# Attention with a three-slot PSUM ring: another order of units, fp32r projections, the rotation as one operation per unit, normalisation on ScalarE

## What is computed

```python
q = (x @ Wq.T + bq)      # 16 heads, two streams of 8 columns each
k = (x @ Wk.T + bk)
v = x @ Wv.T + bv        # 16 heads of 8 columns
q1, q2, k1, k2 = rope of the streams of q and k
a1 = softmax(causal(q1 k1 / sqrt(8))); a2 = softmax(causal(q2 k2 / sqrt(8)))
out = (a1 - lam * a2) @ v
out = out * rsqrt(mean(out * out) + EPS) * head_norm_w * (1 - LAMBDA_INIT)
return out @ Wo.T + bo
```

## Time and profile before

| | |
|---|---|
| median of 3 runs | 1861.6 us (1861.06 to 1861.72) |
| profiled execution: its own time, its span | 1863.3 us, 1861.6 us |
| PE busy (matmul, ends modelled) | 1608.8 us, 86% |
| DVE busy | 1363.2 us, 73% |
| ACT busy | 1269.4 us, 68% |
| POOL busy | 1046.3 us, 56% |
| mean granted TensorE clock | 0.968 of full speed |

### The profile page before, as it was taken

How to read it: one execution, slowest core, us unless ns; L and a number is a source line. 1 busy time by engine, 2 the same in 40 slices (tenths; PEclk the granted TensorE clock), 3 DMA queues, 4 the chain that set the end, 5 groups by cost and what they waited for, 6 DMA issues and landing times. The chain is left out here.

```text
span 1861.6 us, 43161 instructions
## 1 busy us (share of the span) xinstructions
PE 1608.8 (86%) x16448; PEld 1220.1 (66%) x16448; DVE 1363.2 (73%) x3442; ACT 1269.4 (68%) x1613; POOL 1046.3 (56%) x707
## 2 busy tenths in 40 slices
PE   4999999994588888888888888888873799999998
PEld 3787777883466666666666666666652577778787
DVE  5777777765778778878887788788742677777775
ACT  4777777772167767767677677677664577777776
POOL 4888888875324434334344343343312688888885
PEclk9999999997699999999999999999996799999999
DMA  3333323321323233232232332322302232233331
GB/s 113 103 114 115 102 88 108 109 103 46 87 79 92 58 91 82 66 94 72 76 94 61 86 87 60 95 78 70 89 12 77 97 115 90 93 114 110 108 109 63
DMA packets 142846, 163.14 MB, mean 88 GB/s; under 512 B 13244, under 2 KB 124558, under 8 KB 141454
## 3 DMA queue, kind: packets, MB, share of 16 engines
q1 hardware_dynamic: 142640, 160.38, 28.8%
HBM read 91.20 MB, written 14.70 MB: 57 GB/s over the span
## 5 line engine op out<-in xcount | busy, mean ns | idle before, releaser
L292 POOL TENSOR_TENSOR ffn_h_low<-ffn_h,ffn_h_high 128x1024 fp32r<-128x1024 f32 x192 | 458.4, 2401 | 95.0 <-ACT ffn_h_high L341 94.8
L1019 ACT ACTIVATE att_prob<-att_ring 128x1024 f32<-128x1024 f32 x384 | 388.6, 1022 | 155.9 <-PE att_ring L1240 153.4
L1125 DVE TENSOR_REDUCE att_nmax<-att_ring 128x4 f32<-128x1024 f32 (+1 forms) x384 | 450.8, 1217 | 54.3 <-PE att_ring L1240 54.3
L479 DVE TENSOR_TENSOR ffn_h<-ffn_up,ffn_comb_wide 128x1024 f32<-128x1024 f32 x256 | 311.3, 1216 | 125.1 <-ACT ffn_up L334 122.8
L334 ACT ACTIVATE ffn_up<-ffn_up 128x1024 f32<-128x1024 f32 x256 | 258.1, 1008 | 202.8 <-PE ffn_up L567 201.1
L341 ACT ACTIVATE ffn_h_high<-ffn_h 128x1024 fp32r<-128x1024 f32 x256 | 269.3, 1052 | 0.7 <-DVE ffn_h L479 0.7
L935 POOL TENSOR_TENSOR att_qk<-att_turned 128x512 f32<-128x512 f32 x64 | 81.4, 1273 | 318.0 <-DVE att_turned L1104 318.0
L1240 PE MATMUL att_ring<-att_qs,att_kd 64*128 64x256 bf16 (+1 forms) x2048 | 151.1, 249 | 95.4 <-DVE att_nmax L1125 57.2
L567 PE MATMUL ffn_up<-ffn_xt_high,ffn_w_high 128*128 128x512 f32 x512 | 214.7, 419 | 1.7 <-DVE ffn_h L479 1.6
L580 PE MATMUL ffn_y<-ffn_h_high,ffn_w_high 128*128 128x512 f32 x512 | 205.3, 401 | 7.0 <-POOL ffn_h_low L292 6.0
L284 POOL TENSOR_TENSOR ffn_ez<-ffn_e_const,ffn_nz 128x16 f32<-128x16 f32 x64 | 185.6, 2901 | 38.2 <-DVE ffn_nz L405 38.2
(11 more groups left out here) (146 smaller groups left out, 2840.7 us busy)
## 6 DMA issues: line engine op xcount, KB each, us to landing
ffn_comb_wide<-ffn_comb_d SPq DMA_DIRECT2D x128, 512.0 KB, 5.6
att_qs<-att_parts SPq DMA_DIRECT2D x192, 128.0 KB, 2.5
att_kd<-att_parts SPq DMA_DIRECT2D x192, 128.0 KB, 2.5
ffn_x<-x SPq DMA_DIRECT2D x32, 256.0 KB, 3.1
ffn_w<-w SPq DMA_DIRECT2D x4, 1024.0 KB, 7.2
x<-ffn_out SPq DMA_DIRECT2D x16, 256.0 KB, 2.4
att_x<-x SPq DMA_DIRECT2D x32, 128.0 KB, 2.3
att_xr<-x SPq DMA_DIRECT2D x32, 128.0 KB, 2.3
```

The source lines that it names most:

```text
L292: nc.gpsimd.tensor_tensor(hts[1][:, e % NH], h[:, e % NH], hts[0][:, e % NH], ALU.subtract).then_inc(low_by_pool, 1)
L479: nc.vector.tensor_tensor(h[:, e % NH], up[:, e % NUP], comb_wide[:, b.c % NW, e].unsqueeze(1).to_broadcast([P, HE, FT]), ALU.mult).then_i ...
L1019: nc.scalar.activation(prob[:, u % NP], ring[:, ORDER.index((kind, u)) % 3], ACT.Exp, scale=SCALE).then_inc(prob_ready, 1)
L1125: nc.vector.tensor_reduce(nmax[:, b, :, h0:h0 + cnt], ring[:, pos % 3] .rearrange("p (s h k) -> p s h k", s=2, k=width), AX.X, ALU.max, ne ...
```

## The change

It does six things, all in the attention.

1. `ORDER` and the table `AFTER` are written anew. S0, S1 and S2 now stand among XT, QK0 and QK1, NM comes behind S2, OP is last.
2. The projections of q, k and v are three fp32r products each (high x high, high x low, low x high: `PRODUCTS`) in place of one fp32 product. The weights are split once at the start; xt is split in every turn, its high part by ScalarE's copy, its low part by a new VectorE subtraction behind XT.
3. VectorE's rotation is one operation per unit (no bias).
4. The bias, already rotated, lies in `biased`, made once by VectorE at the start, and GpSimd adds it in a second addition behind rotate.
5. ScalarE normalises x, as Identity with scale and bias; VectorE makes the shift (minus mean times rstd) for it.
6. GpSimd's rstd also waits for the normalisation of the turn before, and waits for the new semaphores are added.

```diff
-ORDER = [("XT", 0), ("T", 6), ("QK", 0), ("NM", 0), ("QK", 1), ("S", 0), ("S", 1), ("T", 7), ("T", 8), ("S", 2),
...
+ORDER = [("XT", 0), ("T", 6), ("S", 0), ("QK", 0), ("S", 1), ("QK", 1), ("S", 2), ("NM", 0), ("T", 7), ("T", 8),
+         ("S", 3), ("T", 9), ("S", 4), ("S", 5), ("T", 10), ("T", 11), ("S", 6), ("S", 7), ("T", 0), ("S", 8),
+         ("T", 1), ("V", 0), ("S", 9), ("NT", 0), ("OT", 0), ("NT", 1), ("T", 2), ("S", 10), ("T", 3), ("T", 4),
+         ("S", 11), ("T", 5), ("OP", 0)]
...
-    "streams": ("T", 4), "ms": ("XT", 0), "rms": ("T", 6), "newton": ("S", 1), "scaled": ("T", 0),
-    "stats": ("S", 7), "rstd": ("S", 8), "normalise": ("S", 10),
+    "copy 1": ("S", 4), "copy 2": ("T", 11), "copy 3": ("S", 8), "streams": ("S", 8), "ms": ("XT", 0),
+    "rms": ("QK", 0), "newton": ("S", 2), "scaled": ("T", 0), "stats": ("NM", 0), "rstd": ("T", 7), "shift": ("S", 5),
+    "normalise": ("S", 8),
...
@@ gpsimd
                 def ln_rstd(turn):
                     wait(pool, ln_step, turn.at(2, 3, 3))
+
+                    wait(pool, xn_ready, turn.at(1, 1, 1))
...
-                        nc.gpsimd.tensor_tensor(qk[:, n], turned[:, n, 0], turned[:, n, 1], ALU.add).then_inc(qk_ready, 1)
+                        nc.gpsimd.tensor_tensor(qk[:, n], turned[:, n, 0], turned[:, n, 1], ALU.add).then_inc(rotated, 1)
+                        wait(pool, rotated, turn.at(1, 2, n + 1))
+                        nc.gpsimd.tensor_tensor(qk[:, n], qk[:, n], biased[:, n].rearrange("p c q -> p (c q)"),
+                                                ALU.add).then_inc(qk_ready, 1)
...
@@ scalar
+                act.wait_ge(weights_in, 16 * 12)
+                nc.scalar.activation(wqks[0][:], wqk[:], ACT.Copy).then_inc(weight_high, 1)
+                nc.scalar.activation(wvs[0][:], wv[:], ACT.Copy).then_inc(weight_high, 1)
...
+                def normalise(turn):
+                    wait(act, shift_ready, turn.at(2, 1, 1))
+
+                    wait(act, pe["XT"], turn.at(1, 1, 1))
+                    for t in range(QB):
+                        last = nc.scalar.activation(xn[:, t], x[:, turn.slot(2), t], ACT.Identity, bias=shift[:, t:t + 1],
+                                                    scale=rstd[:, t:t + 1])
+                    last.then_inc(xn_ready, 1)
...
@@ vector
-                            for partner in range(2):
-                                for c in range(2):
...
-                                    last = nc.vector.scalar_tensor_tensor(
-                                        out=turned[:, u, partner, c * S:(c + 1) * S], in0=ring[:, pos % 3, col:col + S],
-                                        scalar=bqk[:, n:n + 1], in1=rope[:, partner], op0=ALU.add, op1=ALU.mult)
-                            last.then_inc(read["QK"], 1)
+                            nc.vector.tensor_tensor(turned[:, u].rearrange("p n (c q) -> p n c q", c=2),
+                                                    ring[:, pos % 3].rearrange("p (n c q) -> p n c q", n=2, c=2),
+                                                    rope[:].unsqueeze(2).to_broadcast([P, 2, 2, S]),
+                                                    ALU.mult).then_inc(read["QK"], 1)
...
+                        if kind == "XT" and turn.runs(1):
+
+                            wait(dve, read["XT"], turn.at(1, 1, 1))
+                            nc.vector.tensor_tensor(xts[1][:], ring[:, pos % 3, 0:S], xts[0][:],
+                                                    ALU.subtract).then_inc(xt_low, 1)
...
+                dve.wait_ge(weight_high, 2)
+                nc.vector.tensor_tensor(wqks[1][:], wqk[:], wqks[0][:], ALU.subtract).then_inc(weight_low, 1)
+                nc.vector.tensor_tensor(wvs[1][:], wv[:], wvs[0][:], ALU.subtract).then_inc(weight_low, 1)
...
@@ tensor
-                                wait(te, read["XT"], turn.at(1, 1, 1))
+                                wait(te, xt_low, turn.at(1, 1, 1))
                                 for n in range(4):
-                                    last = mm(buf[:, n * S:(n + 1) * S], wqk[:, 4 * u + n], xt[:])
+                                    for i, (a1, a2) in enumerate(PRODUCTS):
+                                        last = mm(buf[:, n * S:(n + 1) * S], wqks[a1][:, 4 * u + n], xts[a2][:],
+                                                  start=(i == 0), stop=(i == 2))
```

More of the change, by code:

```diff
@@ L739, in attention @@
         rstd = sb("rstd", [P, QB])
+        shift = sb("shift", [P, QB])
         xn = sb("xn", [P, QB, D])
-        xt = sb("xt", [P, S])
+        wqks = [sb(f"wqk_{n}", [P, 2 * NC4, P], F32R) for n in ("high", "low")]
+        wvs = [sb(f"wv_{n}", [P, D], F32R) for n in ("high", "low")]
+        xts = [sb(f"xt_{n}", [P, S], F32R) for n in ("high", "low")]
         turned = sb("turned", [P, 2, 2, 2 * S])
         qk = sb("qk", [P, 2, 2 * S])
+        biased = sb("biased", [P, 2, 2, S])
         left = sb("left", [P, 2, 2 * S])
@@ L1044, in body @@
                                                  ACT.Copy).then_inc(read["OT"], 1)
+                        if (kind, u) == AFTER["normalise"] and turn.runs(2):
+                            normalise(turn)
                         if kind == "NM" and turn.runs(-1):
@@ L1077, in ln_stats, with mean_shift @@
                     nc.vector.tensor_scalar(var_eps[:], mean_var[:, :, 1], LN_EPS, None, ALU.add).then_inc(ln_step, 1)
-                def normalise(turn):
+                def mean_shift(turn):
                     wait(dve, rstd_ready, turn.at(2, 1, 1))
[L1082 to L1086, removed]
+                    wait(dve, xn_ready, turn.at(1, 1, 1))
+                    nc.vector.scalar_tensor_tensor(out=shift[:], in0=mean_var[:, :, 0], scalar=-1.0, in1=rstd[:],
+                                                   op0=ALU.mult, op1=ALU.mult).then_inc(shift_ready, 1)
                 def body(turn):
@@ L1161, in body @@
                             ln_stats(turn)
-                        if (kind, u) == AFTER["normalise"] and turn.runs(2):
-                            normalise(turn)
+                        if (kind, u) == AFTER["shift"] and turn.runs(2):
+                            mean_shift(turn)
                         if (kind, u) == ("S", 11) and turn.runs(0):
@@ L1202, in _ @@
                                                in1=by_head(0), op0=ALU.add, op1=ALU.subtract).then_inc(lam_step, 1)
+                for u in range(2):
+                    for c in range(2):
+                        last = nc.vector.tensor_scalar(biased[:, u, c], rope[:, 0], bqk[:, 4 * u + c:4 * u + c + 1], None,
+                                                       ALU.mult)
+                last.then_inc(bias_step, 1)
+                dve.wait_ge(bias_step, 1)
+                for u in range(2):
+                    for c in range(2):
+                        last = nc.vector.scalar_tensor_tensor(out=biased[:, u, c], in0=rope[:, 1],
+                                                              scalar=bqk[:, 4 * u + 2 + c:4 * u + 3 + c], in1=biased[:, u, c],
+                                                              op0=ALU.mult, op1=ALU.add)
+                last.then_inc(bias_step, 1)
+                dve.wait_ge(bias_step, 2)
                 dve.wait_ge(lam_step, 3)
+                dve.wait_ge(weight_high, 2)
+                nc.vector.tensor_tensor(wqks[1][:], wqk[:], wqks[0][:], ALU.subtract).then_inc(weight_low, 1)
+                nc.vector.tensor_tensor(wvs[1][:], wv[:], wvs[0][:], ALU.subtract).then_inc(weight_low, 1)
                 dve.wait_ge(v_set, 1)
@@ L1231, in free @@
                         back -= 3
-                    if kind == "T":
+                    if kind == "XT":
+                        wait(te, xt_low, before.at(1, 1, 1))
+                    elif kind == "T":
                         wait(te, prob_ready, before.at(offset(kind, u), 12, u + 1))
```

22 lines of the change are left out of this document (14 added, 8 removed), and 8 rows, old and new, of the table AFTER.

## The result

| | before | after |
|---|---|---|
| median | 1861.7 us (1861.06 to 1862.28) | **1889.5 us** (1885.23 to 1893.0, 4 runs) |
| profiled execution: own time, span | 1863.3, 1861.6 us | 1885.2, 1883.5 us |
| mean granted TensorE clock | 0.968 | 0.950 |

The change is 1.5% slower: ratio 1.0147, 95% interval 1.0128 to 1.0166. The forecast was 1854 with a range of 1812 to 1876, so the prediction is wrong in size and in sign.

The account below looks back on a forecast made before the run. No engine is full, so the loop TensorE to reader to TensorE, or VectorE's 23.1 us a turn, bounds it. Turns of 28.0 for 28.53 us give -15 over 29, first turns +8: 1854 us, range 1812 to 1876.

Parts of the forecast that it names:

- The turn laid out: Schedule of one attention turn from TensorE's start of XT to the next XT: 28.0 us, against 28.53 before.
- weigh 2 (1.5): TensorE's weigh 2 unit, between T11 and S6, takes 1.5 us as in the rows of the kernel before.
- The collision: VectorE's Newton steps wait for GpSimd's second rotation and second bias addition: 1.5 us per turn.
- Rival (a): Newton's steps do not wait for GpSimd's additions: 26.6 us a turn, 1814 us in all; chance 16%.
- The shift: VectorE's new 2-column operation for ScalarE's normalisation: at most one Newton step, 0.2 us.
- The durations: Times assumed per operation: products 0.12 us, QK unit 1.44, two normalisations 0.8 to 0.9, second addition 1.27, rotation 1.13 to 1.15.
- rival (c): TensorE's 256-column products take 0.19 us each, deciding from about 0.14: 29.4 us a turn, 1895 us; chance 6%.
- the page's spacing: Skill page's product spacing, 131 ns at 512 columns: QK unit some 1.2 us, sum about 7 us lower; not adopted.
- rival (b): Late key transfers hold S0, lengthening turns to 28.8 us: 1879 us in all; chance 12%.
- The first turns: At the start, weight split and biased rope cost about 3 us, S0 ahead of QK0 4 to 6: together +8.

Follow-up runs that it names:

- run 1: The changed kernel with 12 unused bf16 products of 256 columns on TensorE ahead of S5: 1862.9 us, ratio 1.000 to the kernel before.
- run 2: The changed kernel with 4 unused products on TensorE ahead of S5: 1872.2 us, ratio 1.0052 to the kernel before.
- run 3: The changed kernel with Newton's steps behind S5 instead of S2, nothing else: 1827.5 us, ratio 0.9811 to the kernel before.
- run 7: The changed kernel with the old tables, all other edits kept, and Newton behind S5 in place of S1: 1869.6 us, ratio 1.0043.
- run 4: The changed kernel without GpSimd's second addition (scores lack the q and k bias), Newton still behind S2: 1822.8 us, ratio 0.9787.
- run 5: The changed kernel with Newton and the statistics behind S5, rstd behind S6 and the shift behind S7: 1828.9 us, ratio 0.9817.
- run 9: The changed kernel with Newton behind S5 and mid 1 behind T0 in place of T1, for earlier key transfers: 1823.8 us, ratio 0.9783.
- run 8: The kernel before with only the new tables (old operations, no second addition, VectorE's normalisation behind S5): 1846.0 us, ratio 0.9903.
- run 6: The changed kernel with ORDER and AFTER as before, shift and normalise both at S10, all other edits kept: 1958.7 us, ratio 1.0524.
- run 10: The changed kernel with Newton behind S5 and single fp32 products for the three fp32r ones, without VectorE's subtraction: 1831.2 us, ratio 0.9829.

## Why the prediction was wrong

**The step that failed** is "The turn laid out", in one term: "weigh 2 (1.5)". It took the duration of a row of before, and with it TensorE's full clock, for a turn in which VectorE holds TensorE up for 1.63 us. In 15 of 28 turns the clock is at half there; they cost 26.7 us. The span was forecast at 1861.6 - 15 + 8, about 1854, and came at 1883.5; the clock is most of the 29 between. By the medians it is 26.6 (1889.5 to 1862.9 in run 1) of 35.5; the other 9 are the first turns and the key waits, below. Runs 1, 2, 3 and 7 show it from four sides: filling the pause, filling a third of it, and twice removing it. No rival of the prediction had it. I had asked what each longer wait does to the slots, not what it does to the engine that waits.

**The collision** was right. Forecast: Newton's first two steps 0.7 and 1.3, 1.5 us per turn. Measured: 0.68, 0.19, 1.13; the second step, forecast at 1.3, isn't held, and the third is. Removing the collision takes 28.00 - 26.76 = 1.24 off the turn, or 1.29 by run 4; run 5, without any collision, gets no further, so another bound is met there and the price may be a little higher. Rival (a), 26.6 a turn without it, is what runs 3 and 4 show: 26.7. The shift, put at "0.2", took 0.85 for the same reason (it starts at 809.76 and ends with the "low" that runs from 809.44 to 810.60); it lay in VectorE's idle time before S6 and cost nothing.

**The turn**: 28.0 forecast, 28.00 in every undisturbed turn. In the turn from 824.90, T11 starts at 13.44 (13.4 forecast), S6 is read at 15.97 (15.9). That it agrees so closely is in part luck: QK0 is read at 3.34 (3.1 forecast), S2's read ends at 7.95 (7.65), and Newton at 10.17 (10.05), so errors of opposite sign cancel. In the long turn S6 is read at 17.63. VectorE's idle time before the first rotation is 0.40 to 0.72 in place of the 2.03 of the earlier trace rows (0.6 forecast).

**The durations**: products of 256 columns every 0.12 us (0.12), as these records of TensorE in the kernel after show:

```profile
797.16 0.28 PE L1288 MATMUL att_ring<-att_xt_low,att_wqk_high 128*128 128x256 f32 x1
797.28 0.28 PE L1288 MATMUL att_ring<-att_xt_high,att_wqk_low 128*128 128x256 f32 x1
```

so rival (c) is out. A whole QK unit takes 1.60 to 1.64 where the prediction had 1.44, since its first product has 0.2 and the unit behind starts 0.2 after its last; the turn came out at 28.00 all the same. V's are 0.11 apart, the normalisation takes 0.87 for two (0.8 to 0.9), the second addition 1.28 to 1.32 (1.27), a rotation 1.14 back to back. Between the row at 512 columns and the page's spacing the row was the right guide: half of 0.23, where "TensorE: Matmul & The Clock Gate" of the Trainium skill (Back-to-back issue gap) would have led to less.

**The keys**, rival (b), happen in part: S0 waited for them 6 times between 600 and 1280 us, 3.8 us in all, 1.0 at most. It is small beside the clock, but it comes next: it hits a third of run 3's turns, and in run 9 it is gone, for 4 us.

**The first turns**: +8 forecast, +8.0 measured at the fourth XT, with the first product at 456.46 (near 456 forecast). The fifth XT is where the steady turns begin: +9.8 there, 11 to 12 in runs 1 and 9. With the old order (run 7) it is +2.8, which fits the split of the weights and the biased rope ("about 3"). But the new order alone, without either, costs 10.9 there (run 8), where the prediction gave it 4 to 6: the two don't add up, and that the fourth XT stands at just +8.0 is luck. So even at full clock the forecast would have been low. In run 1 the first turns cost 11.2, and the 27 turns behind them gain 9.4 in place of some 14, since many have more than 28.0: 1862.9.

**The operations gain only together with the order.** By the table the new order alone takes 1.03 us off the turn. The changed operations save nothing in the old order (28.57 for 28.53) and 0.74 in the new one, but only with Newton moved; at Newton's place in the change they cost 0.50 even at full clock (28.00 for 27.50). That VectorE's saved work counts in the new order because its long wait ahead of the rotation is gone is an argument that no run tests by itself.

## What to carry to other kernels

A small VectorE operation with all inputs in SBUF mostly cost here whatever was left of the GpSimd instruction that it met (0.68 to 1.18 us in place of 0.18). Before adding work to GpSimd, list the small VectorE steps that fall into the same stretch, and move them: one table entry was worth 62 us here. When a change lengthens a wait of TensorE, even in a kernel that keeps it 87% busy, look at the granted clock in windows of a few us behind that wait; the mean over the program moves little (0.950 for 0.968), and the 40 slices don't show it.

## What was not expected of the hardware

- The granted clock fell from 2.4 to 1.2 GHz for about 3 us behind waits of 0.19, 0.41, 1.63 and 0.30 us, with TensorE at work between them. In 12 of 27 turns the same waits left it at 1.00, so equal pauses don't have equal effect. Before, where the longest wait of TensorE for VectorE was 0.77 us, it never fell in the steady turns. "TensorE: Matmul & The Clock Gate" of the Trainium skill (HAM oscillation) describes the fall behind one long wait for a DMA in every pass of a loop; here it came behind a chain of short ones, none over 1.81 us. What exactly the chip weighs these runs don't tell.
- With 4 filler products the clock fell in fewer turns and mostly earlier (S5 at 858.39 already takes 0.61 us), and weigh 2 took 1.9 to 2.4 us, once 2.79; with 12 it didn't fall in the steady turns.
- A VectorE step waited for a GpSimd instruction that had begun, and one that started together with the next instruction wasn't held (0.19 between 0.68 and 1.13). "SBUF — State Buffer" of the Trainium skill (SBUF: two separate sides) describes the shared ports as taken by whichever instruction starts first, for its whole length; the third step agrees (1.13 us, ended within 0.1 of the addition), and operations that read PSUM, such as the maxima at 1.13 to 1.23, were not held.
- The spread of the times was largest where the clock falls in the steady turns: 7.8 us over 4 runs after, 17.5 in run 6, 6.7 in run 2. Where it doesn't, it was 0.4 to 2.9 in runs 3, 4, 5, 7, 8 and 9, but 5.7 in run 10 and 5.8 over the ten of run 1, so the two are not cleanly apart.
